# Issuing the two on-chip copies of V from ScalarE instead of SyncE in a fused attention and feed-forward kernel

## The reference

```python
qkv = h @ wqkv
q, k, v = jnp.split(qkv, 3, axis=-1)
...
bk, bv = (look_around(bk), look_around(bv))   # own window and the one before
sim = jnp.einsum('bhwid,bhwjd->bhwij', bq, bk)
mask = (i < j) | (i > j + WINDOW) | (j == -1)
attn = jax.nn.softmax(sim, axis=-1)
out = jnp.einsum('bhwij,bhwjd->bhwid', attn, bv)
...
x = x + o @ wo
```

## Time and profile before

| what | value |
|---|---|
| median of 3 runs | 2610.24 us (2607.21 to 2612.92) |
| the profiled execution: its time | 2607.61 us |
| the profiled execution: first to last instruction (span) | 2605.8 us |
| TensorE busy | 2554.4 us, 98% |
| VectorE busy | 2200.3 us, 84% |
| ScalarE busy | 2048.0 us, 79% |
| GpSimd busy | 1692.2 us, 65% |

### The profile page before, as it was taken

One profiled execution on the slowest core, in us unless ns is written; L12 is line 12 of the kernel. 1 busy time (PEld: TensorE's weight loads), 2 busy tenths in 40 slices (PEclk: granted clock), 3 DMA queues, 4 the chain that ended last, 5 costly groups with the idle time before them and its releaser, 6 DMA issues.

```text
span 2605.8 us, 65082 instructions
## 1 busy us (share of the span) xinstructions
PE 2554.4 (98%) x21792; PEld 2259.0 (87%) x21792; DVE 2200.3 (84%) x6610; ACT 2048.0 (79%) x5140; POOL 1692.2 (65%) x1850
## 2 busy tenths in 40 slices
PE   8899999999999999999999999999999999999997
PEld 5677788888999989999899998898988898889896
DVE  4778987888888888888888889898998889998885
ACT  5665788788888888888888888888788887888784
POOL 5533864666666666666666677777777767776673
PEclk9999999999999999999999999999999999999999
DMA  9853411111122111111113321122211222112120
GB/s 296 272 166 102 132 38 41 39 48 32 44 59 63 42 38 38 46 44 45 39 33 94 114 54 43 39 54 54 54 43 41 53 54 54 40 42 56 48 54 23
DMA packets 164990, 173.91 MB, mean 67 GB/s; under 512 B 20120, under 2 KB 130224, under 8 KB 163888
## 3 DMA queue, kind: packets, MB, share of 16 engines
q1 hardware_dynamic: 164656, 169.76, 22.6%
HBM read 80.02 MB, written 51.92 MB: 51 GB/s over the span
## 4 chain that ended last, share of the span: by engine, by line
PE 87%; ACT 3%; DVE 3%; issue 2%; DMA 2%; POOL 1%; SPq 1%; DVEq 0%; ACTq 0%; POOLq 0%
PE p_pair L158 17%; PE p_pair L159 14%; PE p_pair L160 14%; PE p_values L2708 8%; PE p_mixed L158 5%; PE p_mixed L160 5%; PE p_mixed L159 5%; PE p_turn L2689 4%; PE p_turn L2664 2%; PE p_turn L2670 2%; PE p_turn L2696 2%; PE p_mixed L2725 1%; PE p_values L518 1%; PE p_mixed L2634 1%; PE p_turn L476 1%
## 5 line engine op out<-in xcount | busy, mean ns | idle before, releaser
L1051 POOL TENSOR_TENSOR inv_norm<-norm_clipped,minus_half 128x8 f32<-128x8 f32 x256 | 441.8, 1726 | 259.9 <-DVE norm_clipped L1876 259.5
L1350 ACT ACTIVATE prob<-prob,least 128x256 f32<-128x256 f32 (+1 forms) x1024 | 495.5, 485 | 21.5 <-DVE least L1912 13.2
L1912 DVE CUSTOM_DVE_ANT_0 prob<-p_pair,mask,inv_norm 128x256 f32<-128x256 f32 (+1 forms) x1024 | 435.1, 460 | 45.3 <-PE p_pair L160 40.5
L158 PE MATMUL p_pair<-hT_h,w_h 128*128 128x256 f32 (+1 forms) x1408 | 412.1, 293 | 3.3 <-DVE hT_l L1971 2.5
L159 PE MATMUL p_pair<-hT_l,w_h 128*128 128x256 f32 (+1 forms) x1408 | 394.8, 280 | 0.0
L160 PE MATMUL p_pair<-hT_h,w_l 128*128 128x256 f32 (+1 forms) x1408 | 394.7, 280 | 0.0
L158 PEld LDWEIGHTS p_pair<-hT_h,w_h 128*128 128x128 f32 (+1 forms) x1408 | 264.2, 188 | 11.6 <-DVE hT_l L1971 2.7
L1085 POOL TENSOR_TENSOR mixed<-prob 128x256 f32<-128x256 f32 x224 | 165.9, 741 | 152.2 <-DVE rinv L1920 87.3
L160 PEld LDWEIGHTS p_pair<-hT_h,w_l 128*128 128x128 f32 (+1 forms) x1408 | 264.7, 188 | 0.0
L1981 DVE SCALAR_TENSOR_TENSOR gated<-p_pair,columns,gelu 128x256 f32<-128x256 f32 (+1 forms) x384 | 181.6, 479 | 97.2 <-ACT gelu L1407 89.7
L159 PEld LDWEIGHTS p_pair<-hT_l,w_h 128*128 128x128 f32 (+1 forms) x1408 | 263.5, 187 | 0.0
(11 more groups left out here) (157 smaller groups left out, 8770.4 us busy)
## 6 DMA issues: line engine op xcount, KB each, us to landing
v_prev_first<-v_own_first SPq DMA_DIRECT2D x256, 128.0 KB, 2.3
x_tile<-x_rows SPq DMA_DIRECT2D x192, 128.0 KB, 2.2
a_wraw<-in_w_all SPq DMA_DIRECT2D x32, 264.0 KB, 4.3
w_high<-a_wraw_h SPq DMA_DIRECT2D x32, 264.0 KB, 3.5
w_low<-a_wraw_l SPq DMA_DIRECT2D x32, 264.0 KB, 4.4
a_x<-in_x SPq DMA_DIRECT2D x32, 256.0 KB, 4.4
x_rows<-a_x SPq DMA_DIRECT2D x64, 128.0 KB, 1.8
x_tile<-x_rows SPq DMA_DIRECT2D x128, 64.0 KB, 2.0
```

The lines of the kernel that those rows point to most:

```text
L158: pe.matmul(out, lh, rh, start=start, stop=False)
L1051: pool.tensor_tensor(r[:, t.slot(2), heads], rt[:, heads], half[:, heads], ALU.pow).then_inc(pool_r[n], 1)
L1350: act.activation(prob[:, h, cols], prob[:, h, cols], ACT.Exp, bias=least[:, h:h + 1], scale=-1.0, accum_out=rsum[:, h:h + 1]).then_inc(act ...
L1912: dve.tensor_tensor_reduce(prob[:, h, cols], p_score[h % 2][:, c0 + cols.start:c0 + cols.stop], mask[:, a.slot(2), cols], r[:, a.slot(2), ...
```

## The change

`copy_v` keeps its waits and its two transfers, but becomes a call of ScalarE's stream. It is taken out of SyncE's order everywhere, and stands in ScalarE's order two calls or so behind the `v_out` of the same tile: in the repeated step two exponentials behind it.

```diff
@@ on_sync: the function and its calls go
-        def copy_v(t):
-
-            if not t:
-                return
-            n, own = t.slot(3), t.slot(4)
-            sp.wait_ge(act_v, t.done(1, 1))
-            need(sp, pe_pv, t.done(4, -8))
-            if t.g < 3:
-                sp.wait_ge(tab_out, 16)
-            source = t if t.first else t.back(1)
-            sp.dma_start(v_mixed[0:D, n], v[half_rows(source, source.slot(2)), source.slot(4)]).then_inc(v_mixed_in[n], 16)
-            after = t.back(-1)
-            sp.dma_start(v_mixed[D:P, n], v[half_rows(t, t.slot(2)), after.slot(4)]).then_inc(v_mixed_in[n], 16)
...
             store_mid(T(6))
-            copy_v(T(4))
             load_shifted(T(6))
             store_x(T(9))
-            copy_v(T(3))
             refill_tables(T(2), 0)
             load_x(T(2))
...
@@ on_scalar: the same function with act for sp, and its calls
+        def copy_v(t):
...
+            act.wait_ge(act_v, t.done(1, 1))
+            need(act, pe_pv, t.done(4, -8))
+            if t.g < 3:
+                act.wait_ge(tab_out, 16)
...
             v_out(T(4))
             exponential(T(5), 4)
             exponential(T(5), 5)
+            copy_v(T(4))
             exponential(T(5), 6)
             exponential(T(5), 7)
             o_high(T(6))
...
             v_out(T(3))
             exponential(T(4), 0)
             exponential(T(4), 1)
+            copy_v(T(3))
             exponential(T(4), 2)
             exponential(T(4), 3)
```

More of the change, by code:

```diff
@@ L1504, in last_steps @@
             exponential(T(116), 1)
+            copy_v(T(117))
             o_high(T(115))
@@ L1637, in last_steps @@
             exponential(T(121), 5)
+            copy_v(T(122))
             o_high(T(120))
@@ L1753, in last_steps @@
             exponential(T(126), 4)
+            copy_v(T(127))
             gelu(Q(122), 0)
@@ L1812, in last_steps @@
             gated_high(Q(126), 5)
-        return namedtuple("Calls", "x_high squares q_high k_high v_out exponential probs_out mixed_out o_high h_high gelu gated_high step last_steps")(x_high, squares, q_high, k_high, v_out, exponential, probs_out, mixed_out, o_high, h_high, gelu, gated_high, step, last_steps)
+        return namedtuple("Calls", "x_high squares q_high k_high v_out copy_v exponential probs_out mixed_out o_high h_high gelu gated_high step last_steps")(x_high, squares, q_high, k_high, v_out, copy_v, exponential, probs_out, mixed_out, o_high, h_high, gelu, gated_high, step, last_steps)
     def on_vector(dve):
@@ L4310, in first_on_scalar @@
     a.probs_out(7, 3, 0, turn[1])
+    t.copy_v(T(0))
     a.exponential(7, 4)
@@ L4332, in first_on_scalar @@
     t.exponential(T(0), 1)
+    t.copy_v(T(1))
     t.exponential(T(0), 2)
@@ L4354, in first_on_scalar @@
     t.o_high(T(0))
+    t.copy_v(T(2))
     t.exponential(T(1), 4)
@@ L4367, in first_on_scalar @@
     t.exponential(T(2), 1)
+    t.copy_v(T(3))
     t.exponential(T(2), 2)
@@ L4390, in first_on_scalar @@
     t.exponential(T(3), 5)
+    t.copy_v(T(4))
     t.exponential(T(3), 6)
@@ L4406, in first_on_scalar @@
     t.exponential(T(4), 3)
+    t.copy_v(T(5))
     t.exponential(T(4), 4)
@@ L4446, in first_on_scalar @@
     t.exponential(T(6), 1)
+    t.copy_v(T(6))
     t.exponential(T(6), 2)
@@ L4463, in first_on_scalar @@
     t.gelu(Q(2), 0)
+    t.copy_v(T(7))
     t.probs_out(T(6), 0)
@@ L4482, in first_on_scalar @@
     t.x_high(T(9))
+    t.copy_v(T(8))
     t.exponential(T(7), 7)
@@ L4507, in first_on_scalar @@
     t.gated_high(Q(2), 4)
+    t.copy_v(T(9))
     t.gated_high(Q(2), 5)
@@ L4520, in first_on_scalar @@
     t.exponential(T(9), 3)
+    t.copy_v(T(10))
     t.probs_out(T(8), 0)
@@ L4547, in first_on_scalar @@
     t.probs_out(T(9), 0)
+    t.copy_v(T(11))
     t.probs_out(T(9), 1)
@@ L4585, in first_on_scalar @@
     t.exponential(T(11), 4)
+    t.copy_v(T(12))
     t.exponential(T(11), 5)
@@ L4597, in first_on_scalar @@
     t.probs_out(T(11), 1)
+    t.copy_v(T(13))
     t.mixed_out(T(11))
@@ L4633, in first_on_scalar @@
     t.exponential(T(13), 3)
+    t.copy_v(T(14))
     t.exponential(T(13), 4)
@@ L4649, in first_on_scalar @@
     t.exponential(T(14), 1)
+    t.copy_v(T(15))
     t.exponential(T(14), 2)
@@ L4684, in first_on_scalar @@
     t.exponential(T(15), 4)
+    t.copy_v(T(16))
     t.exponential(T(15), 5)
@@ L4698, in first_on_scalar @@
     t.q_high(T(17))
+    t.copy_v(T(17))
     t.exponential(T(16), 0)
@@ L4733, in first_on_scalar @@
     t.exponential(T(17), 5)
+    t.copy_v(T(18))
     t.o_high(T(16))
@@ L4747, in first_on_scalar @@
     t.exponential(T(18), 1)
+    t.copy_v(T(19))
     t.exponential(T(18), 2)
```

50 lines of the change are left out of this document (17 added, 33 removed).

## The result

The changed kernel takes 2636.72 us (median of 4 runs, 2634.41 to 2639.44) beside 2610.16 us of the kernel before on the same chip (4 runs, 2607.21 to 2612.92): a ratio of 1.0102, with a 95% interval of 1.0085 to 1.0120. It is about 26.6 us slower (by the interval 22 to 31). The forecast was no measurable change, 2614 us, with a range of its own of 2608 to 2618 and a stated range of 2606 to 2642. The result lies inside the stated range, far outside the forecast's own, and between its two slower rivals, +12 and +53 us.

What follows compares the result with a forecast made beforehand. TensorE, busy 98% of the span, was taken to bound the kernel. First copy 4.2, covered steps 0, second copy 0, ends 2, relief -2.5 made about +3.5: 2614 us beside 2610.24; own range 2608 to 2618, stated 2606 to 2642.

Steps and rivals of the forecast that it cites:

- relief: SyncE freed of 256 issues: loads of x come sooner, ending TensorE's waits for x_tile, -2.5 us.
- ends: Some 26 copies before and behind the steady part, each counted at a quarter of x: 2 us at 0.3.
- second copy: A step's second copy delays gelu and gated, but TensorE's next widen starts 1.15 us later: cost 0 up to 1.15.
- x: How much later ScalarE's third exponential behind v_out starts; taken as 0.3 us, bounds 0 and 1.3.
- half-way rival: Each exponential is handed to ScalarE only as it starts, x = 0.7: together +12, 2622 us; chance 0.22.
- covers of the first copy: Inside a sequence slack of 0.58 and 0.23 us absorbs x; where one begins, none: 14 x 0.3 = 4.2 us.
- length of an issue: On ScalarE's queue the two issues last about 0.47 and 0.6 us, a pair with its gaps 1.21 us.
- full-price rival: The two issues are simply added to ScalarE, x = 1.3: +53, 2663 us; chance 0.2.

Runs made afterwards that it cites:

- behind_fourth: The changed kernel with both copies in the loop's 48 steps moved behind the fourth exponential, directly ahead of o_high: 2629.29 us (1.0077).
- experiment 3: Three kernels: ScalarE makes only each pair's first issue (2607.59 us); changed kernel's loop pairs directly behind v_out (2660.83); or behind the fourth exponential (2629.29).
- experiment 4: The changed kernel with the copies of tiles 0 to 19 and 116 to 127 back on SyncE: 2626.89 us (1.0072).
- no_copies: The kernel before without the copies from the fourth tile on, TensorE's wait for them lowered, output not the reference's: 2608.48 us (1.0000).
- in_gaps: The changed kernel with the loop's copies on ScalarE where it waits for TensorE anyway, the other 32 tiles' back on SyncE: 2607.05 us (0.9994).
- straight_behind: The changed kernel with both copies in the loop's 48 steps directly behind v_out, ahead of the first exponential: 2660.83 us (1.0203).
- loop_only_act: The changed kernel with only the loop's copies left on ScalarE, those of the first 20 and last 12 tiles on SyncE: 2626.89 us (1.0072).
- pool_moved: The changed kernel with GpSimd's two residual_x1 additions moved behind inverse_std(T(5)) in the loop's 48 steps: 2630.80 us (1.0086).

## Why the prediction was wrong, step by step

"No measurable change" was wrong: the interval of 1.0085 to 1.0120 is clear of 1. That 2636.72 us lies inside 2606 to 2642 is owed to the slower rivals that this range was stretched for, not to the forecast's sum, whose relief, ends and second copy failed as well as its x. (The sum's own terms add up to +3.7, not +3.5; nothing hangs on that.)

- **x = 0.3 is the step that failed.** "The stream runs ahead of the engine, so the wait for `v_out` ends at 1358.96" left out that two exponentials stand between `v_out` and the issue, and that each has a wait of its own in the stream. The second one's minimum was read out only at 1373.78 in the step shown of the kernel after, and the issue began at 1373.88:

```profile
1373.70 0.08 DVE L1910 DVE_READ_ACCUMULATOR2_ANT least<- 128x1 f32 x1
```
```profile
1373.88 0.47 ACTq L1326 DMA_DIRECT2D v_prev_first<-v_own_first  x1
1373.92 0.49 ACT L1334 ACTIVATE prob<-prob,least 128x256 f32<-128x256 f32 x1
```

  The even spacing of the exponentials, on which 0.3 rested, says nothing on that: they are indeed handed over before the last has ended, but each only once its minimum is there. In the trace of before the same minimum is there only at 1359.31, 0.35 us behind `v_out`:

```profile
1359.23 0.08 DVE L1912 DVE_READ_ACCUMULATOR2_ANT least<- 128x1 f32 x1
```

  With 0.10 from there to the issue and 1.21 for the pair that gives 0.35 + 0.10 + 1.21 - 0.98 = 0.68, the half-way rival's x. Of the rival's two reasons "such a wait may hold the stream" is right: the stream stops at the first unmet wait. The other, that "each exponential is handed over only as it starts", isn't, by behind_fourth. The Trainium skill, Advanced Engine Details and Errata, Engine Queue Depths, gives ScalarE a queue of 8 instructions, which the forecast cited for a low x. The trace doesn't speak against that queue, but it doesn't help here: with six instructions to hold, the issue still began 0.45 us behind `v_out`, as one of the six lacked its semaphore. Measured x is 0.64, and 0 and 1.2 in the kernels of experiment 3.
- **The covers of the first copy were right, but for one row.** Inside a sequence of the first layer nothing is lost at 0.64 but where a long issue falls, and 0.4 at 1.2; where a new one begins, x is lost nearly whole, 14 times. The path has one more hold than was predicted: `kT_l` and `turn_mixed` make 0.17 us of it, `qT_l` and the turn ahead 0.33, and the prediction didn't look at that pair's slack. This term was sized 4.2 us with x = 0.3; the 14 steps lost 10.3, of which 3.2 in the first and the last of them, and those belong to the ends.
- **"Second copy: 0 up to 1.15" failed**, by a path that the prediction didn't follow. It compared `gated` with TensorE's next `widen` and was right for that, but left out GpSimd behind VectorE, whose shift by 0.3 us made `residual_x1` run into `gT_l` in the second layer, and left out the long issues: 5.2 of 6.9 us go when the additions are moved. Alone, this copy costs 12 us.
- **The ends** were sized 26 x 0.25 x x = 2 us at x = 0.3 and 4.2 at 0.64. The trace has 19 copies outside 510 to 2490 us, not 26. The profile's loss there, 5.4 - 0.2 = 5.2 us, is two fifths of 19 x 0.64 = 12.2, not a quarter; with the first and the last step that begins a sequence it is the 8 us of experiment 4.
- **The relief** was sized -2.5 us. The waits for x_tile did go, but no_copies and in_gaps show no gain that can be told from zero.
- **The length of an issue** was right: medians of 0.468 and 0.620 us on ScalarE beside 0.467 and 0.597 on SyncE. The spread was not weighed. Some issues last over a microsecond on either engine, and on ScalarE they hold everything; the 1.9 us lost in covered steps of the first layer stand where such issues fall.
- The half-way rival had x right and came out at +12 by the sizes above. With the measured sizes its sum is 7.1 for the twelve steps between, 1.9, 6.9 and 8 for the ends, 24 us in all, beside the 26.6 (22 to 31) measured; the profiled execution has the same 24.3 and the 2.5 from before the first copy, which stay open. The full-price rival's +53 us is what straight_behind takes, but with other shares: there the pair was moved, and x is 1.2.

## What to carry to other kernels

A DMA issued by a compute engine costs no busy time in the profile, yet the engine starts nothing behind it until it is over; and the issue itself starts only when every instruction ahead of it has had its semaphores. So read when the wait of the instruction just ahead ends, add the pair's 1.15 us, and see what is due by then. Placed where the engine waits for another one anyway (in_gaps), the same 192 issues are free; behind two exponentials they cost about 19 us (loop_only_act), and directly behind `v_out` most of straight_behind's 53. And check first what the relieved queue can give back: here it was nothing that can be measured.

## What the hardware showed that was not expected

- An issue now and then lasts 1.1 to 2.1 us instead of 0.6. In the steady part of the kernel before, between 1010 and 1514 us, SyncE has one every 71 to 73 us, and in the kernel after some of them fall to ScalarE: at 1676.39, 1823.19, 1969.69 and 2116.91 us, 147 us apart. ScalarE then stands still for the whole of it. They go with the place in the program, not with the time: in the kernel before those of 1153.91, 1297.75 and 1442.15 us are 143.8 and 144.4 apart, four steps each. In straight_behind, whose steps are longer, those of 1173.82, 1320.50 and 1467.38 are 146.7 and 146.9 apart, in the same steps, 6.3 to 6.9 us behind `hT_h` in both. There SyncE's issue of 1173.96 is long as well (1.15 us) beside ScalarE's (1.30). What makes them long stays open.

```profile
1676.39 1.58 ACTq L1328 DMA_DIRECT2D v_prev_first<-v_own_first  x1
1678.02 0.51 ACT L1334 ACTIVATE prob<-prob,least 128x256 f32<-128x256 f32 x1 [1.49 <-issue]
```

- Two `gT_l` of 128x256 take 0.75 us in pool_moved (at 1539.75) and 1.78 in the kernel after (at 1834.36), beside GpSimd's additions, and no row names VectorE as waiting: the contention shows as a longer instruction, not as idle time. It is longest in the steps in which a long issue fell to the second copy.
